# A fused language-model block on one core: zeroing in pieces, router logits side by side in the array, a wider moving operand in the expert down products, and a moved SBUF region

## The chip, the cores and the metric

The kernel runs on one core of one Trainium2 chip. The metric is the device time of one execution in microseconds (us). A time differs by some tenths of a microsecond from one run to the next, so the median of several runs is given.

## The reference, cut to what matters

2048 tokens (2 sequences of 1024), width D = 256. All arithmetic is float32.

```python
q = codebook[x]                                     # gather of 2048 rows of 256
h = gelu(q @ W1 + b1) @ W2 + b2                     # token MLP, 256 -> 1024 -> 256
u = layernorm(h)
for l in range(2):                                  # two minGRU layers, a scan along the sequence
    u = mingru(u, Wz[l], bz[l], Wh[l], bh[l])
h = h + u
y = layernorm(h)
shared = (gelu(y @ w1s) * (y @ w2s)) @ w3s          # a GEGLU that all tokens pass
logits = y @ Wg                                     # 8 experts
e = argmax(logits)                                  # top 1
routed = (gelu(y @ W1[e]) * (y @ W2[e])) @ W3[e]    # one GEGLU of 1024 hidden per token
out = h + shared + routed
```

## The kernel before, in words

**Number format.** Most products are made as three reduced-precision products (`mm3`, L248): each operand is kept as a high part and a low part (fp32r), and the sum is hi*hi + hi*lo + lo*hi. ScalarE (ACT) writes the high part with a copy, VectorE (DVE) the low part with a subtraction. A few products are plain fp32: the transposes against the identity, the router logits (L606) and the two rank products (L615, L616). A plain fp32 product that isn't a transpose shows as two MATMUL instructions in the trace, each with a weight load of its own.

**Tiling.** Tokens go in 4 blocks of 512 (BLOCKS = 4), each of 4 tiles of 128 (BT = 4). The hidden 1024 goes in 8 chunks of 128 (HC = 8). `c` counts chunks through the whole program: 0 to 31 are the token MLP (8 chunks for each block), 32 to 55 the shared GEGLU of blocks 0 to 2, then come the routed tiles, then chunks 56 to 63, the shared GEGLU of block 3. TensorE's loop over `c` (L654 to L691) makes in each turn: the up products of chunk c (12 matmuls over 512 columns for a shared chunk), side work written into tables by chunk number (`X1T`, `UNIT`, `LOG` and so on; a name with `_END` puts the work at the end of the turn), and the down products of chunk c - 2 (12 matmuls over 256 columns). The DVE and ACT programs walk the same chunks and wait for TensorE and for each other by semaphores. The order on each engine is fixed by this text; nothing is planned at run time.

**Router.** For each block the 8 logits of each token are made by `router_logits(b)` (L598 to L608): the tokens (`xlT`, 128 x 128) are the stationary operand, the 8 columns of `wgs` the moving one, into PSUM bank FLIP = 6. `take_logits(b)` (L1152) copies them out on DVE. Bank 6 and 7 are shared by all transposes, so `x1_transposes(3)`, `state_transposes(3)` and `x2_transposes(3)` wait for `logits_taken` 1, 2 and 3. Block 0's logits are made at the end of turn 31, block 1's at the end of 38, block 2's at the end of 41, block 3's in the middle of 43. `choose_experts` (L1175, end of DVE's turn 43) makes the one-hot choice, `rank_products` (middle of TensorE's turn 44) and `place_experts` (DVE's turn 44) the positions. GpSimd scatters the rows into `x_sorted` in DRAM, half of them only after chunk 51's low part.

**Routed tiles.** Tokens sorted by expert fill 16 to 23 tiles of 128; in this data 20 are made. For tile i TensorE's `routed_tile(i)` (L726) makes 8 transposes of the gated tile i - 1 (`g_transposes`), 24 up matmuls over 512 columns (`up_half`, the tokens `xTp` are stationary, the expert's weights move), 2 transposes of the next tile, and the `down` of tile i - 1 (L704): for each of 8 chunks one `mm3` with `gTp` stationary and 256 columns of the third weight moving, all accumulated in `ps[:, 7, 0:256]`. DVE's `take_routed` (L1367) copies these 256 columns to `y_row`, GpSimd scatters them to `y_tokens`. In a tile that is the first of its expert ACT and DVE also split the next expert's three weights (`next_hi`, `next_lo`: 3 x 128 x 2048 each). The weights lie in two slots, each with a high half and, PART elements further on, a low half.

**Queues.** SyncE (SP) issues the weight loads. It also writes zeros to the 25 tiles of `x_sorted` (L303, L304), behind the loads of the shared weights, in one loop without waits between; `normalise(1, 3)` on DVE (turn 35) and GpSimd's `iota` (L408) wait for all of it (`zeroed`). Behind it on SP stands the load of the first expert's first weight (L307), which is wanted by the splitting in turn 44.

**SBUF.** `region()` hands out areas in order. `r_rows` (17 KiB, of which 16 KiB + 96 bytes are used by `xn2` and `zero_row`) stands between `r_xh` and `r_xl`.

Of the kernel before, what the change touches and what calls it, by code (L numbers as in the profile page):

```python
# [5 lines left out]
P = 128  # L6
ALU = mybir.AluOpType
ACT = mybir.ActivationFunctionType
AX = mybir.AxisListType.X
# [10 lines left out]
def build(nc, idx, codebook, tok_w1, tok_b1, tok_w2, tok_b2, gru_wz, gru_bz, gru_wh, gru_bh,  # L20
# [45 lines left out]
    X2T_END = {40: 2}  # L66
    LOG = {43: 3}
    LOG_END = {31: 0, 38: 1, 41: 2}
    RANK = 44
# [12 lines left out]
    with ExitStack() as ctx:  # L82
# [27 lines left out]
        r_xh = region(8)  # L110
        r_rows = region(17)
        r_xl = region(4)
        r_xb = region(8)
        r_gelub = region(2)


# [54 lines left out]
        shift_by = small("shift_by", [P, 1])  # L171
        wgs = small("wgs", [P, KD, EXPERTS])
        stats = small("stats", [P, BT, 6])
# [61 lines left out]
        x2_ps = sem("x2_ps"); xb_hi = sem("xb_hi"); xb_lo = sem("xb_lo"); xl_act = sem("xl_act");  # L235
        logit_ps = sem("logit_ps"); logits_taken = sem("logits_taken"); onehot_steps = sem("onehot_steps"); onehot_done = sem("onehot_done")
        rank_ps = sem("rank_ps"); router = sem("router"); placed = sem("placed"); routed = sem("routed"); scattered = sem("scattered")
# [43 lines left out]
        def _(sp):  # L281
# [4 lines left out]
            sp.dma_start(bh[:], gru_bh).then_inc(small_land, 16)  # L286
            sp.dma_start(wgs[:], wg).then_inc(small_land, 16)
            w2v = tok_w2.rearrange("p k n -> p (k n)")
# [13 lines left out]
            sp.wait_ge(zero_id, 1)  # L302
            with sp.Fori(0, XT + 2) as j:  # L303
                sp.dma_start(x_sorted[bass.ds(j * P, P), :], zero_row[:]).then_inc(zeroed, 16)  # L304

# [131 lines left out]
        def _(pe):  # L437
# [160 lines left out]
            def router_logits(b):  # L598

                pe.wait_ge(xl_act, 2 * b + 2)  # L600
                if b == 0:
                    pe.wait_ge(small_land, 64)
                pe.wait_ge(xb_lo, 2 * b + 2)
                for i in range(BT):
                    for k in range(KD):
                        last = pe.matmul(ps[:, FLIP, i * EXPERTS:(i + 1) * EXPERTS], xlT[:, k, i * P:(i + 1) * P],  # L606
                                         wgs[:, k, :], start=(k == 0), stop=(k == KD - 1))
                last.then_inc(logit_ps, 1)  # L608

            def rank_products():  # L610
# [43 lines left out]
            for c in range(FIRST, AHEAD):  # L654
                if c < MLP:
                    early_down = c % HC == 0 and c > 0
                    if early_down:
                        chunk_down(c - LAG, 0)
                    mlp_up(c)
                else:  # L660
                    early_down = False
                    shared_up(c, 0)
                if c in ST:
                    state_transposes(ST[c])
                if c in X1T:
# [7 lines left out]
                if c == RANK:  # L673
                    rank_products()
                if c == ROW:
                    pe.wait_ge(router, 1)
                    row_transposes(0)
                if c in UNIT:
                    unit(UNIT[c][0])
                if c >= LAG and not early_down:  # L680
                    chunk_down(c - LAG, 0)
                if len(UNIT.get(c, ())) > 1:
                    unit(UNIT[c][1])
                if c in X1T_END:
                    x1_transposes(X1T_END[c])
                if c in ST_END:
                    state_transposes(ST_END[c])
                if c in X2T_END:
                    x2_transposes(X2T_END[c])
                if c in LOG_END:  # L690
                    router_logits(LOG_END[c])  # L691


# [9 lines left out]

            def down(i, slot):  # L704
                for c in range(HC):
                    if c % (HC // NH) == 0:
                        pe.wait_ge(gT_lo, 2 * i + 1 + c // (HC // NH))
                    o = 2 * WCH + c * D
                    last = mm3(pe, ps[:, 7, 0:D], gTp[:, 0, c, :], gTp[:, 1, c, :],
                               w_slots[:, bass.ds(slot + o, D)], w_slots[:, bass.ds(slot + (o + PART), D)],  # L710
                               c == 0, c == HC - 1)
                last.then_inc(tile_done, 1)
# [13 lines left out]
            def routed_tile(i, first_downs=False):  # L726
# [12 lines left out]
                pe.wait_ge(split_lo, last * 3 + 6)  # L739
                down(i - 1, ((last + 1) & 1) * SLOT)  # L740

# [22 lines left out]
            pe.wait_ge(split_lo, 3 * SPLITS)  # L764
            down(back - 1, EXPERTS % 2 * SLOT)
            shared_up(AHEAD + 1, SLOT)
# [223 lines left out]
        def _(dve):  # L990
            dve.memset(zero_row[:, 0:D], 0.0).then_inc(zero_set, 1)
            dve.memset(ones[:], 1.0)
            dve.memset(half[:], 0.5)
            dve.memset(shift_by[:], SHIFT)
# [234 lines left out]
            for c in range(AHEAD):  # L1229
# [12 lines left out]
                if c == 40:  # L1242
                    state_rows(3)
                if c - 1 in LOG_END:
                    take_logits(LOG_END[c - 1])
                if c % HC == LAG + 1 and HC < c < MLP + HC:
# [5 lines left out]
                if c >= MLP:  # L1252

                    shared_gated(c)
                    if c == 32:
                        row_stats(2, 1)
                        row_moments(2, 1)
# [10 lines left out]
                    if c == 41:  # L1268
                        normalise(2, 3)
                chunk_lo(c)  # L1270
                if c == 5:
# [12 lines left out]
                if c in X1T:  # L1284
                    x1_split_lo(X1T[c])
                if c in LOG:
                    take_logits(LOG[c])
                if c in H0:
# [11 lines left out]
                if c == 22:  # L1300
                    row_stats(2, 0)
                    row_moments(2, 0)
                if c == 38:
                    row_stats(2, 2)
                    row_moments(2, 2)
# [6 lines left out]
                for n in SPLIT_PIECES.get(c, ()):  # L1312
                    split_piece_lo(n)
                if c == 43:
                    choose_experts()
                if c == RANK:
# [135 lines left out]
```

## Time and profile before

| | us |
|---|---|
| median of 3 runs (lowest, highest) | 499.87 (499.44, 500.29) |
| the profiled execution, its own time | 499.71 |
| its span in the trace | 498.0 |
| TensorE busy in the span | 490.6 |
| VectorE, ScalarE, GpSimd busy | 320.2, 248.6, 71.2 |

The profile shows one execution. PE is TensorE's matmuls, PEld its weight loads, which overlap the matmuls; DVE is VectorE, ACT ScalarE, POOL GpSimd, SP SyncE. A time that is written L250 belongs to line 250 of the kernel. `mm3` has the three lines L250 (hi*hi), L251 (hi*lo) and L252 (lo*hi), whoever calls it; the names `out<-in` tell which product it is (`ps<-w_slots,gTp` is the down of a routed tile). A matmul's own duration is longer than the distance to the next one, since matmuls overlap in the array: what it costs the engine is the distance between two starts, called pitch below.

### The profile page before, as it was taken

Reading aid. Unit: us, or ns where it says so; the run is one execution under the profiler, and the core shown is the slowest. Engines: PE = TensorE matmul, PEld = TensorE weight load, DVE = VectorE, ACT = ScalarE, POOL = GpSimd, SP = SyncE. Lnnn points to the kernel's source line nnn. Section 1 sums busy time; section 2 is a strip of 40 time slices with the busy share of each in tenths; the row PEclk is TensorE's granted clock in tenths of the full one; section 3 lists DMA queues with packets and bytes.
Section 4 is the critical chain, followed back from the end, with each engine's and each line's share of the span. In section 5 each row is a group of like instructions: output and inputs, shape, how many; then the busy total and the mean of one; then the engine's idle time right before and its main releaser. Section 6 shows DMA issues by size and latency. Waiting matters only on the chain.

```text
span 498.0 us, 9330 instructions
## 1 busy us (share of the span) xinstructions
PE 490.6 (99%) x2946; PEld 434.0 (87%) x2947; DVE 320.2 (64%) x533; ACT 248.6 (50%) x380; POOL 71.2 (14%) x85
## 2 busy tenths in 40 slices
PE   8999999999999999999999999999999999999997
PEld 7889888888888888988888898898898898898886
DVE  2567768668676778657635866833857477557364
ACT  3776774575653553433433765534554457254321
POOL 4431031011011001103460001011001000101110
PEclk9999999999999999999999999999999999999999
DMA  4999010000000004000454465620546084500352
GB/s 132 325 295 239 7 42 1 1 0 2 1 1 1 1 0 168 3 0 33 138 169 108 155 222 205 201 105 32 195 167 227 21 265 133 193 32 32 108 189 84
DMA packets 22857, 52.70 MB, mean 106 GB/s; under 512 B 6096, under 2 KB 16336, under 8 KB 18864
## 3 DMA queue, kind: packets, MB, share of 16 engines
q1 hardware_dynamic: 17168, 42.39, 26.1%
q0 software_dynamic: 2640, 7.22, 4.0%
q10 hardware_dynamic: 3024, 2.75, 1.8%
q8 instruction: 16, 0.26, 0.2%
q14 instruction: 9, 0.07, 0.0%
HBM read 41.85 MB, written 10.51 MB: 105 GB/s over the span
## 4 chain that ended last, share of the span: by engine, by line
PE 94%; DVE 3%; issue 1%; ACT 1%; DVEq 0%
PE ps L250 28%; PE ps L251 28%; PE ps L252 28%; PE ps L719 4%; PE ps L440 2%; PE ps L606 1%; PE ps L624 1%; PE ps L548 1%; PE ps L595 1%; PE ps L583 1%; DVE stats L1080 1%; DVE v_gate L1111 0%; ACT a_gate L867 0%; ACT t_gate L865 0%; ACT v_gate L869 0%
## 5 line engine op out<-in xcount | busy, mean ns | idle before, releaser
L1015 DVE TENSOR_TENSOR hT<-ps,hT 128x512 fp32r<-128x512 f32 x64 | 43.9, 686 | 34.9 <-ACT hT L818 16.6
L1348 DVE TENSOR_TENSOR w_slots<-stage,w_slots 128x2048 f32 x24 | 54.8, 2287 | 15.2 <-ACT w_slots L948 15.1
L250 PE MATMUL ps<-w_slots,xTp 128*128 (+1 forms) x160 | 64.2, 401 | 0.2
L252 PE MATMUL ps<-w_slots,xTp 128*128 (+1 forms) x160 | 62.5, 391 | 0.0
L251 PE MATMUL ps<-w_slots,xTp 128*128 (+1 forms) x160 | 62.2, 389 | 0.0
L422 POOL DMA_INDIRECT y_tokens<-y_row,row_ids x23 | 22.4, 975 | 198.9 <-DVE y_row L1371 188.4
L250 PE MATMUL ps<-w_slots,gTp 128*128 (+1 forms) x160 | 46.8, 293 | 0.0
L818 ACT ACTIVATE hT<-ps 128x512 fp32r<-128x512 f32 x32 | 19.1, 598 | 54.1 <-DVE ps L1021 48.4
L252 PE MATMUL ps<-w_slots,gTp 128*128 (+1 forms) x160 | 45.3, 283 | 0.0
L251 PE MATMUL ps<-w_slots,gTp 128*128 (+1 forms) x160 | 45.2, 283 | 0.0
L1329 DVE TENSOR_TENSOR g_buf<-ps,gelu_buf 128x512 f32<-128x512 f32 x40 | 26.8, 685 | 28.1 <-PE ps L252 28.1
L948 ACT ACTIVATE w_slots<-stage 128x2048 f32 x21 | 40.3, 1917 | 3.9 <-issue 3.9
L1021 DVE TENSOR_TENSOR ps<-ps,gelub 128x512 f32<-128x512 f32 x32 | 22.3, 697 | 30.9 <-PE ps L252 26.0
L972 ACT ACTIVATE gTp<-ps 128x512 fp32r<-128x512 f32 x40 | 21.7, 595 | 39.0 <-PE ps L719 39.0
L802 ACT ACTIVATE ps<-ps,b 128x512 f32<-128x512 f32 x32 | 21.1, 660 | 36.1 <-PE ps L252 36.0
L964 ACT ACTIVATE gelu_buf<-ps 128x512 f32<-128x512 f32 x40 | 23.9, 597 | 29.7 <-PE ps L252 25.3
L814 ACT ACTIVATE gelub<-ps 128x512 f32<-128x512 f32 x32 | 19.2, 600 | 37.5 <-PE ps L252 36.6
L250 PE MATMUL ps<-w2p,hT 128*128 128x256 f32 x128 | 36.8, 288 | 1.0 <-DVE hT L1015 0.7
L250 PE MATMUL ps<-w_slots,hT 128*128 128x256 f32 x128 | 36.5, 285 | 0.0
L252 PE MATMUL ps<-w_slots,hT 128*128 128x256 f32 x128 | 36.2, 283 | 0.0
L251 PE MATMUL ps<-w_slots,hT 128*128 128x256 f32 x128 | 36.2, 283 | 0.0
L252 PE MATMUL ps<-w2p,hT 128*128 128x256 f32 x128 | 36.2, 283 | 0.0
(183 smaller groups left out, 1289.5 us busy)
## 6 DMA issues: line engine op xcount, KB each, us to landing
stage<-ew_in SPq DMA_DIRECT2D x24, 1024.0 KB, 5.0
x_sorted<-zero_row SPq DMA_DIRECT2D x25, 128.5 KB
x_row<-x_sorted ACTq DMA_DIRECT2D x21, 128.0 KB
stage<-w1s_in SPq DMA_DIRECT2D x2, 1024.0 KB, 8.9
fetched<-y_tokens SPq DMA_DIRECT2D x4, 512.0 KB, 5.3
out_rows<-fetched SPq DMA_DIRECT2D x3, 512.0 KB
first_stage<-tok_w_in SPq DMA_DIRECT2D x1, 1024.0 KB, 4.9
first_stage<-tok_w_in SPq DMA_DIRECT2D x4, 256.0 KB
```

Source lines behind the costliest of these rows:

```text
L250: pe.matmul(dst, lhs_hi, rhs_hi, start=start, stop=False, skip_group_check=shares_bank)
L251: pe.matmul(dst, lhs_hi, rhs_lo, start=False, stop=False, skip_group_check=shares_bank)
L252: return pe.matmul(dst, lhs_lo, rhs_hi, start=False, stop=stop, skip_group_check=shares_bank)
L422: pool.indirect_dma_start(out=y_tokens, out_offset=bass.IndirectOffsetOnAxis(ap=row_ids[:, i:i + 1].bitcast(I32), axis=0), in_=y_row[:], i ...
L802: act.activation(bank, bank, ACT.Gelu_apprx_tanh, bias=b1[:, c % HC:c % HC + 1]).then_inc(h_gelu, 1)
L948: act.activation(w_slots[:, bass.ds((e & 1) * SLOT + c * WCH, WCH)], stage[:, c, :], ACT.Copy).then_inc(split_hi, 1)
L964: act.activation(gelu_buf[:, n, :], ps[:, 2 * n, :], ACT.Gelu).then_inc(gelu_done, 1)
L972: act.activation(gTp[:, 0, n * BT:(n + 1) * BT, :].rearrange("p c n -> p (c n)"), ps[:, 4 + n, :], ACT.Copy).then_inc(gT_hi, 1)
L1015: dve.tensor_tensor(hT[:, c % RING, 1, :], ps[:, bank, :], f32(hT[:, c % RING, 0, :]), ALU.subtract).then_inc(h_lo, 1)
L1021: dve.tensor_tensor(bank, bank, gelub[:], ALU.mult).then_inc(s_gated, 1)
L1329: dve.tensor_tensor(g_buf[:, n * NB:(n + 1) * NB], ps[:, 2 * n + 1, :], gelu_buf[:, n, :], ALU.mult).then_inc(g_done, 1)
L1348: dve.tensor_tensor(w_slots[:, bass.ds(to + (PART + c * WCH), WCH)], stage[:, c, :], f32(w_slots[:, bass.ds(to + c * WCH, WCH)]), ALU.subt ...
```

## The change

1. **Zeros.** SP's loop over the 25 tiles is written out; before tile j it waits for `h_lo` = 8 + j (the low part of chunk 7 + j), so that one tile is zeroed for each chunk, 7 to 31.
2. **Logits.** `wgs` gets 32 columns (24 of zeros, one memset on DVE) and becomes the stationary operand; the tokens move, 128 columns at a time. The four tiles of a block go to four groups of 32 columns of the array (`tile_position=(0, 32 i)`), with the loop over the tiles inside the one over k. What comes out is turned (32 i + expert on the partitions, tokens along them). DVE copies it to SBUF (`copy_logits`), TensorE transposes it back (`turn_logits`), DVE takes the 4 x 8 columns (`take_logits`). Blocks 0 and 2 get their logits in the middle of turns 31 and 41 instead of the end, and the turn at the end; block 1 the logits at the end of 38 and the turn in the middle of 39; block 3 the logits in the middle of 43 and the turn at its end. `choose_experts` goes from the end of turn 43 to the start of turn 44 on DVE, `rank_products` from the middle of turn 44 to its end.
3. **Down of a routed tile.** For each of the 8 chunks: one matmul of hi (stationary) with the hi and the lo weights as one moving operand of 2 x 256 columns, into all 512 columns of bank 7, and one of lo with hi, 256 columns, into the first half. DVE sums the two halves with a `tensor_reduce` in place of the copy.
4. **SBUF.** `r_rows` is 16 KiB and stands behind all other regions, followed by 96 bytes.

```diff
-    LOG = {43: 3}
-    LOG_END = {31: 0, 38: 1, 41: 2}
+    LOG = {31: 0, 41: 2, 43: 3}
+    LOG_END = {38: 1}
+    TURN = {39: 1}
+    TURN_END = {31: 0, 41: 2, 43: 3}
...
-        r_rows = region(17)
         r_xl = region(4)
         r_xb = region(8)
         r_gelub = region(2)
+        r_rows = region(16)
+        place[0] += 3 * 32
...
-        wgs = small("wgs", [P, KD, EXPERTS])
+        QUARTER = P // 4
+        wgs = small("wgs", [P, KD, QUARTER])
+        logits_turned = small("logits_turned", [P, P])
...
-            with sp.Fori(0, XT + 2) as j:
-                sp.dma_start(x_sorted[bass.ds(j * P, P), :], zero_row[:]).then_inc(zeroed, 16)
+            for j in range(XT + 2):
+                sp.wait_ge(h_lo, HC + j)
+                sp.dma_start(x_sorted[j * P:(j + 1) * P, :], zero_row[:]).then_inc(zeroed, 16)
...
-                for i in range(BT):
-                    for k in range(KD):
-                        last = pe.matmul(ps[:, FLIP, i * EXPERTS:(i + 1) * EXPERTS], xlT[:, k, i * P:(i + 1) * P],
-                                         wgs[:, k, :], start=(k == 0), stop=(k == KD - 1))
+                for k in range(KD):
+                    for i in range(BT):
+                        rows = slice(i * QUARTER, (i + 1) * QUARTER)
+                        last = pe.matmul(ps[rows, FLIP, 0:P], wgs[:, k, :], xlT[:, k, i * P:(i + 1) * P], start=(k == 0),
+                                         stop=(k == KD - 1), tile_position=(0, i * QUARTER))
                 last.then_inc(logit_ps, 1)
+            def turn_logits(b):
+                pe.wait_ge(logits_copied, b + 1)
+                pe.transpose(ps[:, FLIP, 0:P], logits_turned[:], ident[:]).then_inc(turned_ps, 1)
...
-            def down(i, slot):
+            w_parts = w_slots[:].rearrange("p (s h n) -> p s h n", s=2, h=2)
+            def down(i, side):
...
-                    last = mm3(pe, ps[:, 7, 0:D], gTp[:, 0, c, :], gTp[:, 1, c, :],
-                               w_slots[:, bass.ds(slot + o, D)], w_slots[:, bass.ds(slot + (o + PART), D)],
-                               c == 0, c == HC - 1)
+                    pe.matmul(ps[:, 7, :].rearrange("p (h n) -> p h n", h=2), gTp[:, 0, c, :],
+                              w_parts[:, bass.ds(side, 1), :, o:o + D].rearrange("p s h n -> p (s h) n"),
+                              start=c == 0, stop=False, skip_group_check=True)
+                    last = pe.matmul(ps[:, 7, 0:D], gTp[:, 1, c, :], w_slots[:, bass.ds(side * SLOT + o, D)], start=False,
+                                     stop=c == HC - 1, skip_group_check=True)
...
+            def copy_logits(b):
+                dve.wait_ge(logit_ps, b + 1)
+                dve.tensor_copy(logits_turned[:], ps[:, FLIP, 0:P]).then_inc(logits_copied, 1)
             def take_logits(b):
-                dve.wait_ge(logit_ps, b + 1)
-                dve.tensor_copy(logits[:, b * BT:(b + 1) * BT, :].rearrange("p t e -> p (t e)"),
-                                ps[:, FLIP, 0:BT * EXPERTS]).then_inc(logits_taken, 1)
+                dve.wait_ge(turned_ps, b + 1)
+                dve.tensor_copy(logits[:, b * BT:(b + 1) * BT, :],
+                                ps[:, FLIP, 0:P].rearrange("p (t e) -> p t e", e=QUARTER)[:, :, 0:EXPERTS]).then_inc(logits_taken, 1)
...
-                dve.tensor_copy(y_row[:], ps[:, 7, 0:D]).then_inc(y_taken, count)
+                dve.tensor_reduce(y_row[:], ps[:, 7, :].rearrange("p (h n) -> p n h", h=2), AX, ALU.add).then_inc(y_taken, count)
```

On DVE, `copy_logits` stands behind `shared_gated` and ahead of `chunk_lo` in turns 41 and 43, ahead of `chunk_lo` in turn 31, and behind the scan of unit 15 and ahead of `row_stats(2, 2)` in turn 38. `take_logits` stands at the start of turns 32, 42 and 44, as before, and for block 1 behind `shared_gated(39)`, where it stood ahead of it.

## Rows read from the trace of the kernel before

**Rows 1.** The page: busy time of each engine.
```profile
PE 490.6 (99%) x2946; PEld 434.0 (87%) x2947; DVE 320.2 (64%) x533; ACT 248.6 (50%) x380; POOL 71.2 (14%) x85
```

**Rows 2.** The page: the chain that ended last, by engine.
```profile
PE 94%; DVE 3%; issue 1%; ACT 1%; DVEq 0%
```

**Rows 3.** Waits of the whole span: who for whom, total us, times, longest.
```profile
PE ps L250 <- issue: 0.9, 1, 0.9
```

**Rows 4.** PE's groups by form: count, then busy us, mean ns, idle before.
```profile
L250 PE MATMUL ps<-w_slots,gTp 128*128 x152 | 44.6, 293 | 0.0
```

**Rows 5.** Timeline of PE, one routed tile: start us, us, instruction.
```profile
353.04 1.04 PE L719 MATMUL ps<-ident,g_buf 128*128 128x128 f32 x8
...
354.14 0.39 PE L251 MATMUL ps<-w_slots,xTp 128*128 x1
...
359.15 0.39 PE L252 MATMUL ps<-w_slots,xTp 128*128 x1
...
359.84 0.28 PE L252 MATMUL ps<-w_slots,gTp 128*128 x1
...
362.36 0.28 PE L252 MATMUL ps<-w_slots,gTp 128*128 x1
...
362.48 1.03 PE L719 MATMUL ps<-ident,g_buf 128*128 128x128 f32 x8
```

**Rows 6.** Timeline of DVE in the same tile.
```profile
355.76 0.42 DVE L1371 COPY y_row<-ps 128x256 f32<-128x256 f32 x1
...
359.49 1.28 DVE L1329 TENSOR_TENSOR g_buf<-ps,gelu_buf 128x512 f32<-128x512 f32 x2
```

**Rows 7.** Timeline of PE around block 1's logits, turns 38 and 39.
```profile
188.07 1.84 PE L606 MATMUL ps<-wgs,xlT 128*128 128x8 f32 x16
189.78 0.49 PE L250 MATMUL ps<-xb_first,w_slots 128*128 128x512 f32 x1
...
192.64 0.28 PE L250 MATMUL ps<-w_slots,hT 128*128 128x256 f32 x1
...
194.07 1.03 PE L583 MATMUL ps<-ident,hs 128*128 128x128 f32 x8
```

**Rows 8.** Timeline of PE around the rank products, turn 44.
```profile
219.78 0.38 PE L615 MATMUL ps<-onehot,before 128*128 128x128 f32 x2
219.99 0.39 PE L616 MATMUL ps<-onehot,ones 128*128 128x128 f32 x2
220.14 0.36 PE L250 MATMUL ps<-w_slots,hT 128*128 128x256 f32 x1
220.34 0.28 PE L251 MATMUL ps<-w_slots,hT 128*128 128x256 f32 x1
```

**Rows 9.** Timeline of DVE, end of turn 38 and turn 39.
```profile
190.51 1.28 DVE L1128 TENSOR_TENSOR_SCAN hs<-a_gate,carry,v_gate 128x512 f32<-128x512 f32 x1
...
193.28 0.16 DVE L1154 COPY logits<-ps 128x32 f32<-128x32 f32 x1
193.36 0.69 DVE L1021 TENSOR_TENSOR ps<-ps,gelub 128x512 f32<-128x512 f32 x1
```

**Rows 10.** Timeline, turn 41: block 2's second low part, then PE's chunk_down.
```profile
202.04 0.69 DVE L1145 TENSOR_TENSOR xb_third<-ps,xb_third 128x512 fp32r<-128x512 f32 x1 [0.28 <-ACT xlT L891]
...
202.77 0.28 PE L250 MATMUL ps<-w_slots,hT 128*128 128x256 f32 x1
```

**Rows 11.** Timeline of SP's queue.
```profile
18.19 24.01 SPq L304 DMA_DIRECT2D x_sorted<-zero_row  x25
42.40 0.34 SPq L307 DMA_DIRECT2D stage<-ew_in  x1
```

**Rows 12.** Busy us by stretch: PE, PEld, DVE, ACT, POOL, clock, DMA, GB/s.
```profile
18.00:24.00 6.00, 6.00 (x44) 5.62 (x44) 4.28 (x7) 4.85 (x9) 2.25 (x6) 1.00 1.02 405
```

**Rows 13.** Waits of the whole span: ACT's for the load of w1s.
```profile
ACT w_slots L850 <- DMA stage<-w1s_in: 2.2, 1, 2.2
```

**Rows 14.** The view of one line, VectorE's reduction of the logits: min/median/max ns.
```profile
L1179 DVE TENSOR_REDUCE best<-logits x1: 288/288/288, 216.3 to 216.3; 128x16 f32<-128x128 f32 x1
```

More of the change, by code:

```diff
@@ L235, in build @@
         x2_ps = sem("x2_ps"); xb_hi = sem("xb_hi"); xb_lo = sem("xb_lo"); xl_act = sem("xl_act");
-        logit_ps = sem("logit_ps"); logits_taken = sem("logits_taken"); onehot_steps = sem("onehot_steps"); onehot_done = sem("onehot_done")
+        logit_ps = sem("logit_ps"); logits_copied = sem("logits_copied"); turned_ps = sem("turned_ps"); logits_taken = sem("logits_taken"); onehot_steps = sem("onehot_steps"); onehot_done = sem("onehot_done")
         rank_ps = sem("rank_ps"); router = sem("router"); placed = sem("placed"); routed = sem("routed"); scattered = sem("scattered")
@@ L286, in _ @@
             sp.dma_start(bh[:], gru_bh).then_inc(small_land, 16)
-            sp.dma_start(wgs[:], wg).then_inc(small_land, 16)
+            sp.dma_start(wgs[:, :, 0:EXPERTS], wg).then_inc(small_land, 16)
             w2v = tok_w2.rearrange("p k n -> p (k n)")
@@ L672, in _ @@
                     q_transposes(QT[c])
-                if c == RANK:
-                    rank_products()
                 if c == ROW:
@@ L677, in _ @@
                     row_transposes(0)
+                if c in TURN:
+                    turn_logits(TURN[c])
                 if c in UNIT:
@@ L691, in _ @@
                     router_logits(LOG_END[c])
+                if c in TURN_END:
+                    turn_logits(TURN_END[c])
+                if c == RANK:
+                    rank_products()
             def up_half(i, slot, n):
@@ L739, in routed_tile @@
                 pe.wait_ge(split_lo, last * 3 + 6)
-                down(i - 1, ((last + 1) & 1) * SLOT)
+                down(i - 1, (last + 1) & 1)
             chunk_down(AHEAD - 2, 0)
@@ L764, in _ @@
             pe.wait_ge(split_lo, 3 * SPLITS)
-            down(back - 1, EXPERTS % 2 * SLOT)
+            down(back - 1, EXPERTS % 2)
             shared_up(AHEAD + 1, SLOT)
@@ L992, in _ @@
             dve.memset(ones[:], 1.0)
+            dve.memset(wgs[:, :, EXPERTS:QUARTER], 0.0)
             dve.memset(half[:], 0.5)
@@ L1243, in _ @@
                     state_rows(3)
-                if c - 1 in LOG_END:
-                    take_logits(LOG_END[c - 1])
+                if c - 1 in TURN_END:
+                    take_logits(TURN_END[c - 1])
+                if c == RANK:
+                    choose_experts()
                 if c % HC == LAG + 1 and HC < c < MLP + HC:
@@ L1254, in _ @@
                     shared_gated(c)
+                    if c in LOG:
+                        copy_logits(LOG[c])
+                    if c in TURN:
+                        take_logits(TURN[c])
                     if c == 32:
@@ L1269, in _ @@
                         normalise(2, 3)
+                elif c in LOG:
+                    copy_logits(LOG[c])
                 chunk_lo(c)
@@ L1285, in _ @@
                     x1_split_lo(X1T[c])
-                if c in LOG:
-                    take_logits(LOG[c])
                 if c in H0:
@@ L1302, in _ @@
                     row_moments(2, 0)
+                if c in LOG_END:
+                    copy_logits(LOG_END[c])
                 if c == 38:
@@ L1313, in _ @@
                     split_piece_lo(n)
-                if c == 43:
-                    choose_experts()
                 if c == RANK:
```

## The prediction

> **What bounds the kernel now.** The page comes first: TensorE (PE) is busy 490.6 of 498.0 us [rows 1] and holds 94% of the chain that ended last [rows 2]. DVE, the next engine, has 64%. The waits view says how much PE stands still: its longest wait behind the start is 0.9 us once [rows 3], and in the routed part it hardly waits at all. So the end moves with the PE time that an edit saves or costs, and with any wait that it puts into PE's queue; work on another engine counts only if PE comes to wait for it. Next, the timeline gives the price of PE's instructions, which is the pitch from start to start and not the duration in the groups view (293 ns for a down matmul [rows 4]). In one routed tile [rows 5], 22 pitches of 512-column matmuls lie between 354.14 and 359.15: 0.228 us each. 21 pitches of 256-column matmuls lie between 359.84 and 362.36: 0.120 us each. A tile takes 362.48 - 353.04 = 9.44 us.
>
> The sum is made against the profiled execution, 499.71 us (its span is 498.0, the other 1.7 us lie around it and aren't touched). The median of the runs, 499.87, lies 0.16 above; I add that at the end. The runs differ by about 0.4 us either way, so I call a change within 0.2% (1.0 us) no change.
>
> **Down of a routed tile.** 160 chunks (152 + 8 of the other form [rows 4], 20 tiles x 8). Before, a chunk costs 3 x 0.120 = 0.360 us; after, 0.228 + 0.120 = 0.348. What goes is one weight load with its matmul, but not the columns: 768 before, 768 after. Only the fixed part of a pitch is saved, 0.012 us, x 160 = **2.0 us gained**. No row shows the two sizes in alternation. Bounds: 0 gained, if the two-run operand costs what two instructions cost (0.240 for 0.228), and twice my value, if the shorter matmul hides its fixed part too: 0.120 - 0.012 = 0.108, the nearest being the 0.105 us of a plain pass of 128 columns below. I take 2.0 because both sizes stand in the rows with the same fixed part (0.228 = 2 x 0.120 - 0.012).
>
> DVE's copy of 256 columns (0.42 us [rows 6]) becomes a reduction over 512 inputs. Nearest rows: 0.29 us for 128 inputs [rows 14], 0.64 for 512 inputs (two in 1.28 [rows 6]); read with a stride it may be double. So 0.2 to 0.9 us more for each tile. The cover: in this tile, where DVE also splits weights, the gated halves end at 359.49 + 1.28 = 360.77, PE wants the first at 362.48 [rows 5, 6], 1.7 us later. With the reduction at its worst 0.8 us are left. Cost 0; if DVE were 2 us slower, each of the seven such tiles would pay.
>
> **Logits: what goes.** A block's 16 instructions start at 188.07 and the next matmul at 189.78 [rows 7]: 1.71 us, 0.107 each, for 8 columns each; the weight load of 128 columns sets this pace, not the columns.
>
> **Logits: what comes.** Again 16 instructions (4 tiles x 2 k x 2 passes), 128 columns each, with a weight load of 32 columns. A plain fp32 pass of 128 columns over the full array: 219.78 to 219.99 for two, 0.105 us [rows 8]. If nothing runs side by side, the group is 16 x 0.107 = 1.7 us, as before. If the four column groups overlap fully it is 4 x 0.105 + some issue time, about 0.5 us. I take what lies between: PE starts its instructions in order, the two passes of one product follow each other on the same columns, and only the second pass of one tile and the first of the next lie side by side. That makes 8 products x 0.105 + 0.105 = 0.95, rounded up to **1.0 us**. Then the transpose back: 0.11 us and the 0.08 that the first matmul behind such work takes longer (0.20 between its start and the next, for 0.120 [rows 8]): **0.19 us**. Net gain 1.71 - 1.00 - 0.19 = **0.52 us a block**, where no wait comes in.
>
> The Trainium skill (TensorE: Matmul & The Clock Gate, "Packing small matmuls") reports 2.38x for three column tiles side by side. The same section says that a weight load overlaps running matmuls only where its row group differs, and all four tiles here have all the rows. By the first sentence the group would cost an estimated 1.71 / 2.38 = 0.7 us, by the second it is serial or worse. No row here shows either.
>
>
> **Logits: the waits that come.**
> - Block 1. The turn waits for `copy_logits(1)`, which DVE makes behind the scan of unit 15, over at 191.79 [rows 9]: copied by about 192.05. PE gets to the turn at 192.64 - 0.71 = 191.93, so it waits 0.1. Then 0.19 for the turn and 1.43 for chunk_down (194.07 - 192.64 [rows 7]): PE is at `state_transposes(3)` at 193.7. This waits for `logits_taken` 2, and `take_logits(1)` now stands behind `shared_gated(39)` on DVE. Before, the take began at 193.28 and the gating at 193.36 [rows 9]; now the copy delays the statistics by 0.2, the take that goes gives back 0.08, and the gating starts at 193.5, is over at 194.15, and the take ends near 194.3. PE starts the transposes at about 194.3 instead of 194.07: a loss of **0.23 us**, not a gain. Queued behind it on PE are all later chunks.
> - Block 2. Its logits now come right behind `shared_up(41)`, at 202.77; the low part is ready at 202.04 + 0.69 = 202.73 [rows 10]. With the semaphore 0.05 us of waiting: gain **0.47**.
> - Blocks 0 and 3: the low part is done more than 2 us earlier; between logits and turn lies a chunk_down of 1.43 us, in which DVE copies 128 columns (between 0.16 for 32 columns [rows 9] and 0.42 for 256 [rows 6]). Gain 0.52 each.
> - `choose_experts` in turn 44 takes its 1.6 us while PE makes 2.7 us of up products; `rank_products` at the end of the turn come 1.4 us later, but DVE isn't free for `place_experts` before that anyway. 0. Without that cover the scatter would start later, and its second half waits for chunk 51 in either kernel.
>
> Sum: 0.52 + 0.52 + 0.47 - 0.23 = **1.3 us gained**; serial groups and full overlap below give the two ends.
>
> **Zeros and SBUF.** The 25 issues take SP from 18.19 to 42.2 [rows 11]. No wait of PE names a DMA, and with the DMA engines full (405 GB/s) PE is busy 6.00 of 6.00 us [rows 12]. The only early wait for a load that could reach PE is ACT's 2.2 us for w1s [rows 13], and the zeros stand behind that load in the same queue; if they disturbed it all the same, at most PE's 0.9 us [rows 3] would go. I take 0. The load that now stands behind the last zeroed tile (L307 [rows 11]) moves from 42.4 to about 138 and is wanted for the splitting in turn 44, which ends behind the rank products of 219.78 [rows 8]: covered. A zeroed tile for each chunk is done long before `normalise(1, 3)`, three chunks after the last. The moved region changes addresses only; no row prices that, and I take 0.
>
> **The sum:** 499.71 - 2.0 - 1.3 = 496.4; as a median 496.4 + 0.16 = 496.6 us.
>
> **The rivals.**
> - A, the forecast: **496.6**, own range 495.8 to 497.4. Chance 0.45.
> - B, the column groups don't overlap: 16 x 0.107 and 0.19 more, -0.19 for each of 4 blocks, = 0.8 us lost: 499.87 - 2.0 + 0.8 = **498.7**. For it: in every row here one matmul's columns follow another's. Against it: the loads are a quarter as wide, so that their pace (0.107) is gone. Chance 0.25.
> - C, full overlap: a group of 0.5, net gain 1.02, 1.02 and 0.97 for blocks 0, 3 and 2, still -0.23 for block 1, which is tied to DVE: 499.87 - 2.0 - 2.8 = **495.1**. Chance 0.16.
> - D, slower: in the logits each instruction waits until the one before has left the array, because weights go into a part of it that shares its rows. The duration of a 128-column matmul is then its pitch: 0.39 - 0.105 = 0.28 us alone [rows 8]. 16 x 0.28 = 4.5, 3.0 more than before a block with the turn, 12 in all: 499.87 - 2.0 + 12 = **510**. It turns the sum where a group costs 1.71 - 0.19 + 2.0 / 4 = 2.0 us, a pitch of 0.126. Against it: a full load hides behind a running matmul everywhere in this trace. Chance 0.05.
> - E, the 512-column run is split and saves nothing, logits as in A: 499.87 - 1.3 = **498.6**. Chance 0.05. The last 0.04 are for what I haven't seen.
>
> **How the numbers follow.** Faster (under 498.9): all of A and C, two thirds of B and E: 0.81. Same: 0.12. Slower: 0.07. The range 494.9 to 498.9 takes in A, C, most of B and E.
>
> **What would show it.** In a routed tile: starts 0.228 and 0.120 us apart in the down, a tile of 9.34 us, PE without waits. In the logits: 16 instructions in 1.0 us (1.7 means B, 0.5 C, over 2.0 D). A wait of about 0.6 us ahead of `state_transposes(3)`, with DVE as its releaser. The early gap of 0.9 us on PE is still there. I am wrong if the alternation of 512 and 256 columns has a pitch of its own, if the reduction takes over 2 us, or if one of the moved waits is longer than a chunk_down.

## The result, and the profile after

The changed kernel takes 494.62 us in the median (494.06 to 495.23, 6 runs); the kernel before, run beside it, 499.55 (498.73 to 500.29, 6 runs). The ratio is 0.9902, 95% interval 0.9888 to 0.9916: 4.9 us or 1.0% faster. The forecast was 496.6 with a range from 494.9 to 498.9. The direction is right, but the gain was forecast as 3.3 us, and the result lies 0.3 us below the range.

The profiled execution took 494.67 us with a span of 492.9, which is 5.0 us less than the span before (497.97 and 492.94 before rounding). Its page, busy time and chain of waits, for [rows 1, 2]:

```profile
PE 485.4 (98%) x2790; PEld 419.5 (85%) x2791; DVE 326.5 (66%) x538; ACT 248.9 (50%) x380; POOL 71.7 (15%) x85
...
PE 86%; DVE 4%; DMA 4%; ACT 3%; issue 2%; SPq 1%; POOL 0%; POOLq 0%; DVEq 0%
```

PE is busy 5.2 us less, with 156 matmuls fewer: 160 of the down went, four turns came. It is still the engine that sets the end. To find where the time went, the span is cut at landmarks that both kernels have on PE: the first product of turn 32 (on `xb_first`), the first up product of the first routed tile, and the first product of chunk 56 (on `xb_last`). Worked out from the timelines, in us:

| stretch | before | after | gained |
|---|---|---|---|
| start to turn 32 (block 0's logits in it) | 139.22 | 137.57 | 1.65 |
| turn 32 to first routed tile (blocks 1 to 3) | 130.34 | 128.85 | 1.49 |
| the 20 routed tiles, to chunk 56 | 188.79 | 186.92 | 1.87 |
| the rest | 39.6 | 39.6 | 0.0 |

In the 14 profiles of this case the second and third stretch come back to within 0.25 us for kernels that share the code there. The first doesn't: it lies between 137.02 and 138.13 for the eight kernels with the new logits and between 138.34 and 139.22 for before, the region alone and the down alone. Most of that comes ahead of turn 8, where the first product starts between 33.93 and 35.13 us (35.13 before, 34.41 after). From there to turn 32 it is 103.99 to 104.13 us in the six profiles with the old logits and 103.09 to 103.22 in the eight with the new ones. So of the 1.65 us, 0.9 are block 0's logits and 0.7 came ahead of turn 8. What a small edit is worth ahead of turn 8 needs timed runs.

**Logits.** PE's timeline at block 0, turn 31 (start us, us, instruction):

```profile
135.11 0.39 PE L260 MATMUL ps<-qTp,w1p 128*128 128x512 f32 x1
135.43 0.65 PE L618 MATMUL ps<-xlT,wgs 128*32 128x128 f32 x16
136.00 0.39 PE L258 MATMUL ps<-w2p,hT 128*128 128x256 f32 x1
```

The 16 instructions hold PE for 136.00 - 135.43 = 0.57 us, against 1.71 [rows 7] and 1.0 forecast. The instruction ahead has 0.32 to the group's start and not the 0.228 of [rows 5], so about 0.09 us goes for the change of tile size. Behind the group the next matmul takes 0.10 us longer than usual, where it was 0.08 behind the old one. The single starts in the trace come in fours: each four within 0.02 us, the second four 0.13 us behind the first, the third and fourth 0.11 us apart, the last start at 0.37 us. With 0.105 us for one pass [rows 8], that is full overlap, rival C. The turn costs 0.11 us in blocks 0, 2 and 3, and 0.17 in block 1. By how far PE is ahead of the kernel before at the same products, group and turn together give 0.92, 0.91 and 0.91 us in blocks 0, 2 and 3; block 1's group alone gives 1.03.

**Block 1's waits.** PE's timeline of turns 38 and 39:

```profile
186.50 0.64 PE L618 MATMUL ps<-xlT,wgs 128*32 128x128 f32 x16
187.07 0.50 PE L258 MATMUL ps<-xb_first,w_slots 128*128 128x512 f32 x1
...
190.36 0.33 PE L624 MATMUL ps<-ident,logits_turned 128*128 128x128 f32 x1 [0.23 <-DVE logits_turned L1181]
190.44 0.36 PE L258 MATMUL ps<-w_slots,hT 128*128 128x256 f32 x1
...
192.72 1.06 PE L593 MATMUL ps<-ident,hs 128*128 128x128 f32 x8 [0.61 <-DVE logits L1185]
```

and DVE's in the same stretch, for [rows 9]:

```profile
188.84 1.28 DVE L1155 TENSOR_TENSOR_SCAN hs<-a_gate,carry,v_gate 128x512 f32<-128x512 f32 x1
190.04 0.27 DVE L1181 COPY logits_turned<-ps 128x128 f32<-128x128 f32 x1
190.22 1.40 DVE L1107 BATCH_NORM_STATS2 stats<-res 128x6 f32<-128x256 f32 x4
...
191.81 0.68 DVE L1048 TENSOR_TENSOR ps<-ps,gelub 128x512 f32<-128x512 f32 x1
192.39 0.18 DVE L1185 COPY logits<-ps 128x32 f32<-128x32 f32 x1
```

The copy out of PSUM stands behind the scan, so the turn waits for it; the take stands behind the gating (L1048), so the eight `state_transposes(3)` wait for that. Pitches that are too long by 0.39 and 0.76 us come from this, with the turn 1.34 us in all: more than the 1.03 that the shorter group gives. Block 1 loses 0.3 us net, near the 0.23 that was forecast, and both releasers are the forecast ones. The four blocks together give 2.4 us.

**Down.** PE's timeline of one routed tile, for [rows 5]:

```profile
349.45 1.03 PE L745 MATMUL ps<-ident,g_buf 128*128 128x128 f32 x8
...
356.35 0.40 PE L733 MATMUL ps<-w_slots,gTp 128*128 x1
356.58 0.28 PE L736 MATMUL ps<-w_slots,gTp 128*128 x1
356.70 0.40 PE L733 MATMUL ps<-w_slots,gTp 128*128 x1
...
358.70 0.28 PE L736 MATMUL ps<-w_slots,gTp 128*128 x1
358.82 1.03 PE L745 MATMUL ps<-ident,g_buf 128*128 128x128 f32 x8
```

From transposes to transposes the tile takes 358.82 - 349.45 = 9.37 us instead of 9.44. The run of 512 columns (L733) takes 0.236 us from start to start on average, not 0.228, and the 256 behind it (L736) 0.118. So 0.006 us is saved a chunk, not 0.012. A tile saves 0.067 us, 0.05 of it in the down and the rest in its up products, and 20 tiles 0.067 x 20 = 1.34 us. The other 0.5 us of the third stretch is a gap behind the last tile. Before, PE's timeline had it there:

```profile
456.76 0.28 PE L252 MATMUL ps<-w_slots,gTp 128*128 x1
457.51 0.76 PE L719 MATMUL ps<-ident,g_buf 128*128 128x128 f32 x5 [0.47 <-issue]
```

After, the same two places follow each other at the usual pitch:

```profile
452.43 0.28 PE L736 MATMUL ps<-w_slots,gTp 128*128 x1
452.55 0.71 PE L745 MATMUL ps<-ident,g_buf 128*128 128x128 f32 x5
```

The releaser "issue" means that PE waited for nothing that the profile shows. PE's sequencer was late here: by its branches in the trace it spends 2.7 us (454.74 to 457.40 before, 449.54 to 452.19 after) on passes of the tile loop that are skipped, and the transposes before start 0.11 us behind that. Meanwhile PE works off what is already in its queue. Before, that was used up at 456.76 + 0.12 = 456.88, ahead of the sequencer's return; after, it lasts to 452.43 + 0.12 = 452.55, past the return. In both traces 17 matmuls start between the moment the sequencer turns to these passes and the transposes; after, eight of them have 512 columns. So the same number of longer instructions holds more work, which fits; the depth itself was not varied.

**DVE's reduction**, by its line (min/median/max ns):

```profile
L1408 DVE TENSOR_REDUCE y_row<-ps x20: 680/691/693, 284.2 to 459.7; 128x256 f32<-128x512 f32 x20
```

0.69 us for the 0.42 of [rows 6], and no wait of PE names it.

### The profile page after: what moved, and what is told of

It reads as the page before. It is cut to its first block, busy times and chain, and to the rows that moved or that the text cites. A ratio compares the mean times of both kernels' runs of the same rounds, so it can differ in the third digit from the quotient of the medians.

```text
span 492.9 us, 8768 instructions
## 1 busy us (share of the span) xinstructions
PE 485.4 (98%) x2790; PEld 419.5 (85%) x2791; DVE 326.5 (66%) x538; ACT 248.9 (50%) x380; POOL 71.7 (15%) x85
## 4 chain that ended last, share of the span: by engine, by line
PE 86%; DVE 4%; DMA 4%; ACT 3%; issue 2%; SPq 1%; POOL 0%; POOLq 0%; DVEq 0%
PE ps L258 23%; PE ps L259 22%; PE ps L260 22%; PE ps L733 8%; PE ps L736 4%; PE ps L745 3%; DMA stage<-w1s_in 2%; PE ps L640 1%; DVE stats L1107 1%; PE ps L558 1%; DMA q<-codebook_in,idx_sb 1%; PE ps L593 1%; PE ps L605 1%; DVE v_gate L1138 1%; ACT a_gate L893 1%
## 5 line engine op out<-in xcount | busy, mean ns | idle before, releaser
L733 PE MATMUL ps<-w_slots,gTp 128*128 (+1 forms) x160 | 58.9, 408 | 0.0
L736 PE MATMUL ps<-w_slots,gTp 128*128 (+1 forms) x160 | 44.9, 281 | 0.0
L1048 DVE TENSOR_TENSOR ps<-ps,gelub 128x512 f32<-128x512 f32 x32 | 22.3, 697 | 26.9 <-PE ps L260 26.9
L258 PE MATMUL ps<-w2p,hT 128*128 128x256 f32 x128 | 36.9, 288 | 1.0 <-DVE w2p L1053 0.7
L260 PE MATMUL ps<-w2p,hT 128*128 128x256 f32 x128 | 36.2, 283 | 0.0
L259 PE MATMUL ps<-w2p,hT 128*128 128x256 f32 x128 | 36.2, 283 | 0.0
```

The costliest lines, as they stand in the source:

```text
L258: pe.matmul(dst, lhs_hi, rhs_hi, start=start, stop=False, skip_group_check=shares_bank)
L259: pe.matmul(dst, lhs_hi, rhs_lo, start=False, stop=False, skip_group_check=shares_bank)
L260: return pe.matmul(dst, lhs_lo, rhs_hi, start=False, stop=stop, skip_group_check=shares_bank)
L733: pe.matmul(ps[:, 7, :].rearrange("p (h n) -> p h n", h=2), gTp[:, 0, c, :], w_parts[:, bass.ds(side, 1), :, o:o + D].rearrange("p s h n - ...
L736: last = pe.matmul(ps[:, 7, 0:D], gTp[:, 1, c, :], w_slots[:, bass.ds(side * SLOT + o, D)], start=False, stop=c == HC - 1, skip_group_chec ...
L1048: dve.tensor_tensor(bank, bank, gelub[:], ALU.mult).then_inc(s_gated, 1)
```

## The experiments

Each ratio is against the kernel before on the same chip.

**The zeros alone.** The kernel before, with this edit and nothing else:

```diff
-with sp.Fori(0, XT + 2) as j:
-    sp.dma_start(x_sorted[bass.ds(j * P, P), :], zero_row[:])...
+for j in range(XT + 2):
+    sp.wait_ge(h_lo, HC + j)
+    sp.dma_start(x_sorted[j * P:(j + 1) * P, :], zero_row[:])...
```

> The kernel before with the zeros alone issued one tile for each chunk; nothing else is changed. Theory 1 (the zeros stood in the way of the loads): w1s lands about 0.7 us earlier than the 27.4 us of before, PE's gap at turn 8 (1.09 us over the pitch, before) shrinks to 0.4 to 0.8 us, the time falls by 0.3 to 0.8 us. Rival (the gap at turn 8 differs from run to run only): w1s lands at 27 to 27.5 us and the time is that of before within 0.3 us.

Measured: 498.63 us, 0.9989 (0.9978 to 0.9999). A small gain, barely clear of 1; repeated below. w1s is there at 26.27 us, and PE's gap at turn 8 is gone and not only smaller.

**The down alone.** The kernel before with the new `down` and the reduction:

```diff
-mm3(pe, ps[:, 7, 0:D], ..., c == 0, c == HC - 1)
+pe.matmul(ps[:, 7, :]..., gTp[:, 0, c, :], w_parts[...])
+pe.matmul(ps[:, 7, 0:D], gTp[:, 1, c, :], w_slots[...])
...
-dve.tensor_copy(y_row[:], ps[:, 7, 0:D])
+dve.tensor_reduce(y_row[:], ps[:, 7, :]..., AX, ALU.add)
```

> The kernel before with the down of the routed tiles alone changed, the sum of the two halves on DVE included. Theory 1: pitches of 0.235 and 0.117 us, a tile of 9.37 us for 9.44 (1.3 us in 20 tiles), and the gap of 0.5 us behind the last tile is gone, since PE's queue holds more time: 1.9 us in all, 497.7. Rival (the gap went for another reason, say the logits or the changed phase): the gap stays and the gain is 1.3 us, 498.3.

Measured: 497.59 us, 0.9965 (0.9951 to 0.9978). Turn 32 to the first routed tile is 130.33, as before; the tiles take 186.92, as after. All of the third stretch is this edit. Its tiles alternate, though: 9.33 and 9.41 us in turn, with pitches of 0.231 and 0.116 in the shorter ones and those of the changed kernel in the longer. The mean is 9.37, as in the changed kernel, where every tile takes that. The gap behind the last tile is gone here too, in PE's timeline:

```profile
455.54 0.28 PE L715 MATMUL ps<-w_slots,gTp 128*128 x1
455.66 1.03 PE L724 MATMUL ps<-ident,g_buf 128*128 128x128 f32 x8
```

**The old zeros in the changed kernel.** The first diff turned round:

```diff
-for j in range(XT + 2):
-    sp.wait_ge(h_lo, HC + j)
+with sp.Fori(0, XT + 2) as j:
```

> The changed kernel with the old loop of zeros. Theory 1 (the zeros stood in the way): 0.3 to 0.8 us slower than the changed kernel, 495.0 to 495.4, w1s lands at about 27.4 us and PE's gap at turn 8 is about 1.1 us. Rival: 494.6 as the changed kernel, gap 0.8 us or less.

Measured: 495.04 us, 0.9912 (0.9897 to 0.9926), 0.4 us above the changed kernel (of another series), with intervals that overlap. w1s is there at 26.75 us and PE's wait at turn 8 is 0.56 us: neither the 27.4 us nor the gap of 1.1 that theory 1 wanted. The time points the way the first one does and settles nothing by itself.

**The down undone in the changed kernel:**

```diff
-pe.matmul(ps[:, 7, :]..., gTp[:, 0, c, :], w_parts[...])
-pe.matmul(ps[:, 7, 0:D], gTp[:, 1, c, :], w_slots[...])
+mm3(pe, ps[:, 7, 0:D], ..., c == 0, c == HC - 1)
```

> The changed kernel with the old down of the routed tiles: logits, zeros and region stay changed. Theory 1 (the logits' groups overlap fully and pay 0.9 to 1.0 us a block, block 1 loses 0.3): the logits give 2.4 us, with the start of the program 2.4 to 3.2, so 496.4 to 497.1; tile of 9.44 us and the gap of 0.5 us behind the last tile back. Rival (part of the gain comes from how the edits meet): outside 496.0 to 497.5.

Measured: 496.35 us, 0.994 (0.9926 to 0.9954). The tiles take 189.03, the middle stretch 128.83 as after, and the gap is back, in the waits of PE (who for whom, total us, times, longest):

```profile
PE ps L593 <- DVE logits L1180: 0.6, 1, 0.6
PE ps L740 <- issue: 0.5, 1, 0.5
```

Logits, zeros and region together give 0.6%, the down 0.35% by itself: 0.95% of the 0.98% measured. The parts add up, within the intervals.

**The changed kernel once more**, on the chip of the next three:

```diff
(no edit)
```

> The changed kernel once more, as it is, to stand beside the others of this series. Both theories: 494.3 to 495.0 us. It gives a second landing time of w1s with the new zeros: 26.0 to 26.8 us if the zeros set it, up to 27.5 if it differs from run to run only.

Measured: 494.68 us, 0.9903 (0.9886 to 0.9919), with the middle stretch at 128.83 and the tiles at 187.04.

**Block 1's waits taken away.** On DVE the copy moves ahead of the scan of unit 15, and the take ahead of `row_stats(2, 2)`, where the copy stood:

```diff
 unit_value(u)
+if u == UNITS - 1:
+    copy_logits(1)
 unit_scan(u)
...
-    copy_logits(LOG_END[c])
+    take_logits(LOG_END[c])
 row_stats(2, 2)
...
 shared_gated(39)
-take_logits(1)
```

> The changed kernel with three lines of DVE moved in turn 38: block 1's logits are copied ahead of the scan of unit 15, and taken behind it, ahead of the row statistics and of shared_gated(39). Theory 1 (PE's two waits in turn 39, 0.39 us ahead of the turn and 0.76 us ahead of the state transposes, are DVE's order alone): both go, 1.0 us faster than the changed kernel, 493.6. Rival (behind them the next wait comes up, the scan itself or x2's chain, so that the gain is given back by chunk 41): under 0.4 us faster, 494.3 to 494.6, with new waits of PE between 192 and 200 us.

Measured: 494.01 us, 0.9886 (0.9869 to 0.9902), 0.7 us under the changed kernel on the same chip. With four runs each the two intervals overlap, so the gain rests on the middle stretch, 128.02 instead of 128.83, which elsewhere comes back to within 0.06 us. DVE's timeline shows the new order, PE's what it brings:

```profile
189.27 0.28 DVE L1181 COPY logits_turned<-ps 128x128 f32<-128x128 f32 x1
189.47 1.27 DVE L1155 TENSOR_TENSOR_SCAN hs<-a_gate,carry,v_gate 128x512 f32<-128x512 f32 x1
190.83 0.19 DVE L1185 COPY logits<-ps 128x32 f32<-128x32 f32 x1
...
193.87 0.69 DVE L1042 TENSOR_TENSOR hT<-ps,hT 128x512 fp32r<-128x512 f32 x1 [0.66 <-ACT hT L844]
```

```profile
190.53 0.27 PE L624 MATMUL ps<-ident,logits_turned 128*128 128x128 f32 x1
190.55 0.36 PE L258 MATMUL ps<-w_slots,hT 128*128 128x256 f32 x1
...
192.07 1.04 PE L593 MATMUL ps<-ident,hs 128*128 128x128 f32 x8
...
194.10 0.40 PE L260 MATMUL ps<-xb_second,w_slots 128*128 128x512 f32 x1
194.61 0.50 PE L258 MATMUL ps<-xb_second,w_slots 128*128 128x512 f32 x1
```

Neither the turn nor the state transposes wait. Of the 1.2 us that went (0.39, 0.77 and some of the turn), 0.4 comes back at 194.10: the pitches are 0.51 and 0.34 and not 0.23, because chunk 39's low part on DVE is now what is late.

**The order of the loops in the logits:**

```diff
-for k in range(KD):
-    for i in range(BT):
+for i in range(BT):
+    for k in range(KD):
```

> The changed kernel with the loop over the four tiles outside the loop over k in the router logits. Theory 1 (each group of 32 columns works through its own products by itself, whatever the order they are issued in): a group of 16 instructions still takes 0.5 us from the first to the last start, 494.6 in all. Rival (starts are in order, and the overlap comes from the order of the loops): the four passes of one tile follow each other, only the last lies beside the next tile's first, about 1.4 us a group; 3 us slower in all, 497.5 to 498.

Measured: 494.33 us, 0.9897 (0.988 to 0.9913), no difference. In PE's timeline the group takes 136.44 - 135.84 = 0.60 us:

```profile
135.84 0.67 PE L618 MATMUL ps<-xlT,wgs 128*32 128x128 f32 x16
136.44 0.39 PE L258 MATMUL ps<-w2p,hT 128*128 128x256 f32 x1
```

In this order the four instructions for the same 32 columns are issued one after another. By the forecast's rule only the last of a tile and the first of the next could lie side by side, and the group would take (16 - 3) x 0.105 = 1.4 us. All the same the 16 starts span 0.39 us, in fours as before. A rule of starts in the order of issue, with a pass of 0.105 us on each column group, can't give that: each column group works off its own products, whatever order they are issued in.

**The down's long product from one run.** The moving operand of L733 reads 512 neighbouring columns, not two runs of 256, so the routed part of the result is another:

```diff
-w_parts[:, bass.ds(side, 1), :, o:o + D].rearrange(...)
+w_slots[:, bass.ds(side * SLOT + min(o, 3 * WCH - 2 * D), 2 * D)].rearrange(...)
```

> The changed kernel with the 512 moving columns of the routed down read as one run of 512 (the high halves of two neighbouring chunks) and not as two runs of 256 that lie apart; the routed part of the result is therefore another. Theory 1 (the second run's start costs the 0.007 us by which the wide matmul's pitch is above 0.228): pitch 0.228 and 0.120, a tile of 9.34 us, 0.6 us faster than the changed kernel. Rival (the alternation of 512 and 256 columns has this pitch, whatever is read): pitch 0.235 and 0.117 as before, 9.37, same time.

Measured: 494.9 us, 0.9912 (0.9896 to 0.9929). The pitches in PE's timeline are the same, 0.236 and 0.118 on average, and the tile takes 9.37 us:

```profile
357.04 0.40 PE L733 MATMUL ps<-w_slots,gTp 128*128 x1
357.28 0.28 PE L736 MATMUL ps<-w_slots,gTp 128*128 x1
357.39 0.40 PE L733 MATMUL ps<-w_slots,gTp 128*128 x1
```

The two-run read costs nothing. What is above the forecast comes with the alternation of sizes, but not always: the shorter tiles of `d1` have 0.231 + 0.116 = 0.347, the forecast's 0.348, with the same instructions. What sets the one or the other wasn't looked for.

**The zeros alone again**, the same edit on another chip with the next two:

```diff
+    sp.wait_ge(h_lo, HC + j)
```

> The kernel before with the zeros alone one tile for each chunk, once more, beside the next two. Theory 1 (the early zeros cost something real): again 0.3 to 0.8 us faster than before. Rival (chance of the runs): within 0.2 us of before, w1s landing anywhere between 26.3 and 27.4 us.

Measured: 498.89 us, 0.9987 (0.9979 to 0.9996), 12 runs against 29. With the first, 0.5 to 0.6 us gained, both times just clear of 1.

**The zeros in one burst, only later:**

```diff
+sp.wait_ge(h_lo, HC)
 with sp.Fori(0, XT + 2) as j:
```

> The kernel before with one wait ahead of the old loop of zeros: all 25 tiles go in one burst, but only once chunk 7's low part is done (about 36 us), when the first loads have landed. Theory 1 (what counts is that no zeros are in the queues while w1s, w2s and w3s land): the same gain as with one tile for each chunk, 0.3 to 0.8 us. Rival A (what counts is the spreading): no gain. Rival B (no effect of the zeros at all): no gain in either.

Measured: 498.98 us, 0.9992 (0.9984 to 1.0001). It lies between, 0.1 us from one and 0.5 from the other. If the gain is real here too, it comes from the zeros being out of the loads' way and not from their being spread; this can't be told from no gain.

**The odd-sized region of SBUF moved, and nothing else:**

```diff
-        r_rows = region(17)
...
+        r_rows = region(16)
+        place[0] += 3 * 32
```

> The kernel before with the SBUF region alone moved behind the others. Theory 1 (addresses don't count): the time of before within 0.2 us, tile of 9.44 us. Rival (the start of the program or DVE gets faster by the new places): 0.3 to 0.7 us faster, with shorter instructions on DVE or ACT to be seen in the groups.

Measured: 499.51 us, 1.0 (0.9991 to 1.0009). Nothing.

To see whether the zeros reach PE through the load of w1s, ACT's timeline of that wait, here in the kernel before, then with the zeros alone (`z1`, then `z1b`) and with the region alone (`r1`, old zeros):

```profile
27.42 0.63 ACT L850 ACTIVATE w_slots<-stage 128x512 fp32r<-128x512 f32 x1 [2.23 <-DMA stage<-w1s_in]
```

```profile
26.27 0.63 ACT L851 ACTIVATE w_slots<-stage 128x512 fp32r<-128x512 f32 x1 [1.94 <-DMA stage<-w1s_in]
```

```profile
26.63 0.63 ACT L851 ACTIVATE w_slots<-stage 128x512 fp32r<-128x512 f32 x1 [1.98 <-DMA stage<-w1s_in]
```

```profile
26.14 0.63 ACT L851 ACTIVATE w_slots<-stage 128x512 fp32r<-128x512 f32 x1 [2.07 <-DMA stage<-w1s_in]
```

How this load reaches PE the traces show. Behind its wait for w1s, ACT works in the order of its program, with three pauses of 0.03 us, up to the high part of block 1's `qTp`. DVE makes the low part, and PE's first product of turn 8 reads it. Here are ACT, DVE and PE in the kernel before, then PE in the changed kernel, where the releaser is named:

```profile
33.56 1.08 ACT L797 ACTIVATE qTp<-ps 128x512 fp32r<-128x512 f32 x2
34.31 1.28 DVE L1010 TENSOR_TENSOR qTp<-ps,qTp 128x512 fp32r<-128x512 f32 x2
35.13 0.47 PE L250 MATMUL ps<-qTp,w1p 128*128 128x512 f32 x1 [0.93 <-issue]
```

```profile
34.41 0.47 PE L258 MATMUL ps<-qTp,w1p 128*128 128x512 f32 x1 [0.61 <-DVE qTp L1037]
```

The distance from ACT's first copy of w1s to this product is 35.13 - 27.42 = 7.71 us before and 34.41 - 26.69 = 7.72 after. It is 7.71 or 7.72 in ten of the 14 profiles, all those in which PE waits there. In the other four (`r1`, `z3`, `a1`, `f2`) PE doesn't wait, and the distance is 8.1 to 8.5. So the 0.9 us of [rows 3] is a wait for w1s, handed on by ACT and DVE, and the 0.7 us that the profile of the changed kernel gained ahead of turn 8 is the earlier landing of this load (27.42 - 26.69).

Whether the zeros set the landing is another matter. On average the load is there at 26.9 us in the four profiles with the old zeros and at 26.5 in the nine with zeros for each chunk, but the two sets overlap: 26.14 to 27.42 and 25.60 to 27.20. Counted from the issue of the load it is 11.6 to 13.0 and 11.8 to 12.9 us. That step fits the timed gain and is not shown.

**The statistics moved too.** The kernel with the waits taken away, and `row_stats(2, 2)` with its moments behind the gating:

```diff
-row_stats(2, 2); row_moments(2, 2)      # end of turn 38
 ...
 shared_gated(39)
+row_stats(2, 2); row_moments(2, 2)
```

> The kernel with the mended waits, and the row statistics of block 2 put behind shared_gated(39) on DVE, where they lie beside ACT's copy. Theory 1 (the 0.29 us that PE then waited in the middle of turn 40 was chunk 39's chain on DVE, held up by these statistics): that wait goes, 0.3 us faster than the mended kernel, 493.7. Rival (the statistics are now late for block 2's normalisation): a wait of PE ahead of x2_transposes(2) at about 197.5 us, no gain or a loss.

Measured: 493.76 us, 0.9885 (0.9872 to 0.9899). The wait in turn 40 is gone, but the middle stretch is 128.15, no better than 128.02. In PE's timeline the time comes back at the transposes of x2 and at block 2's logits:

```profile
196.30 1.07 PE L605 MATMUL ps<-ident,xn 128*128 128x128 f32 x8
...
200.29 0.65 PE L618 MATMUL ps<-xlT,wgs 128*32 128x128 f32 x16 [0.15 <-DVE xb_third L1172]
```

Their pitches are 0.28 and 0.22 us longer than in `f1`. DVE is busy 15.1 of the 17.0 us from 185 to 202 in `f1`, 89% against 66% of the changed kernel's whole span, so it fits that DVE fills turns 38 to 41 and the wait only moves. Both mended kernels are the fastest of this case, 5.3 and 5.7 us under the kernel before; from each other the runs can't tell them.

## Why the prediction missed

- **The logits' group: the step that failed.** "PE starts its instructions in order, the two passes of one product follow each other on the same columns, and only the second pass of one tile and the first of the next lie side by side": 1.0 us. The last clause is false, all four tiles lie side by side throughout, and `o1` goes against the first one across column groups. Measured 0.57, with 0.09 ahead of it, against rival C's 0.5. Under C the forecast was 1.02, 1.02 and 0.97 gained for blocks 0, 3 and 2; measured 0.92, 0.91 and 0.91. C as a whole gives 495.1. The evidence against the chosen rule wasn't in any row; what was wrong was to give it 0.45 against 0.16 as a compromise between two ends, and a range that ended at 494.9, just behind C.
- **The turn:** 0.19 forecast, 0.11 measured in three blocks. The 0.08 that the next matmul takes longer is there, but from the transpose to that matmul it is 0.03 us and not 0.11.
- **Block 1:** right in both waits and their releasers. The net, -0.23 forecast, is -0.3. That it is tied to DVE, so that it couldn't profit from the shorter group, is what `f1` shows.
- **Block 2:** right; it waits for nothing in the changed kernel.
- **Down:** 2.0 forecast. The tiles give 1.34, since the pitches are 0.236 and 0.118 (sum 0.354) and not 0.348. The sign of the error was named ("the alternation of 512 and 256 columns has a pitch of its own"). The 0.5 us behind the last tile wasn't seen: it stood in the waits view before as `PE ps L719 <- issue`, and the working didn't ask what a deeper queue does to it. By luck the two nearly cancel, 1.87 for 2.0.
- **The reduction:** right, 0.69 us within 0.2 to 0.9 more and hidden.
- **Zeros:** 0 forecast, 0.5 to 0.6 measured (`z1`, `z1b`). That no wait of PE names a DMA excluded too much: PE's 0.9 us in turn 8 is the wait for w1s, handed on by ACT and DVE. The bound named (0.9) held. Why the zeros would hold that load up stays open.
- **SBUF region:** right, 0.

In the profiles the logits give 2.4 us, the down 1.9 and the stretch ahead of turn 8 0.7: the 5.0 us between the spans. Against the forecast of 496.6 the median is 2.0 us lower. 1.1 of it are the logits (2.4 for 1.3) and 0.5 the zeros; another 0.3 is that the kernel before ran at 499.55 beside it and not at 499.87. The down takes 0.1 back, and 0.2 is left, within the scatter of the runs. So the miss is mainly one mis-sized term, with one that was put at nothing.

The Trainium skill's 2.38x for three column tiles (TensorE: Matmul & The Clock Gate, "Packing small matmuls") would have given an estimated 1.71 / 2.38 = 0.7 us a group. The trace comes near it, with another number of tiles: 0.57 + 0.09 = 0.66 us, or 2.6x, with four. The same section's sentence that a weight load overlaps running matmuls only where its row group differs isn't borne out: all four tiles have all rows, and in the trace the weight loads of the second four start 0.03 to 0.05 us behind the group's first matmul, while the first four run.

## What to carry to other kernels

When small products are put into separate 32-column groups, count the columns of one group alone, in whatever order they are issued. Then look at what the new hand-over (copy, turn, take) waits for on the engine that carries it: here, for one block in four, it took more than the packing gave, and two moved lines brought that stretch 0.8 us. In the waits before, look behind each wait for "issue". One of the two here hung on how much work lay queued ahead of it, the other on a load that PE never names, two engines back.

## What the hardware showed that wasn't expected

- Four 32-column tiles: four starts within 0.02 us (0.04 with the tiles outside), 0.11 to 0.13 us from one four to the next, nearly the same with either loop order (0.37 and 0.39 us for 16 starts). Going over to them costs about 0.09 us.
- 512- and 256-column products in alternation: mostly 0.236 and 0.118 us, against 0.228 and 0.120 in runs of one size, with two runs of 256 or one of 512 alike; 0.231 and 0.116 in every second tile of `d1`.
- A reduction over two PSUM halves with a stride of 256 elements, 512 inputs: 0.69 us, like the 0.69 for an elementwise operation over 512 columns [rows 9]. No cost of the stride shows.
- Skipped passes at the end of PE's tile loop hold its sequencer for 2.7 us, and the queue covers all but 0.5 us of it or all of it, by what lies in it.
